# The last tile of a layer gets its own staging buffers and a 53-partition store, in a three-layer GNN kernel on one core

## What is computed

```
for l in range(3):
    ht  = einsum('nd,rdo->nro', h, W_rel[l])              # a table of 16 rows per node
    h_rel = segment_sum(ht[src, etype], dst) + h @ W_loop[l] + b_rel[l]
    z = h @ W_gat[l];  el = sum(z*attn_l);  er = sum(z*attn_r)      # per head
    e = leaky_relu(el[src] + er[dst]);  alpha = softmax over the edges of dst
    h_gat = segment_sum(alpha * z[src], dst) + b_gat[l]
    hc = concat(h_rel, h_gat) @ W_fuse + b_fuse
    if l == 0: hc = hc * sigmoid(concat(hc, mean weight) @ W_gate + b_gate)
    h = relu(hc)
out = layernorm(x + h)
```

## Time and profile before

| | us |
|---|---|
| median of 3 runs (3658.16 to 3663.75) | 3663.73 |
| the profiled execution | 3656.87 |
| its span in the trace | 3655.3 |
| POOL busy / DVE busy | 2529.9 / 2408.4 |
| ACT busy / PE busy | 430.8 / 688.1 |

### The profile page before, as it was taken

One profiled execution on the slowest core, in us unless ns is written; L12 is line 12 of the kernel. 1 busy time (PEld: TensorE's weight loads), 2 busy tenths in 40 slices (PEclk: granted clock), 3 DMA queues, 4 the chain that ended last, 5 costly groups with the idle time before them and its releaser, 6 DMA issues.

```text
span 3655.3 us, 19643 instructions
## 1 busy us (share of the span) xinstructions
PE 688.1 (19%) x1896; PEld 364.2 (10%) x1896; DVE 2408.4 (66%) x3225; ACT 430.8 (12%) x844; POOL 2529.9 (69%) x2681
## 2 busy tenths in 40 slices
PE   6750111122212221011111112121000000000000
PEld 5420000011101110000000001010000000000000
DVE  6505767677666763676667756673676777877786
ACT  4350011111111111010111111111000000000000
POOL 0057777777777764777777777774777777777774
PEclk9885555555555555555555556565555555555555
DMA  5694454454445553555445445554533333333332
GB/s 203 233 357 99 128 150 150 150 150 150 150 150 160 161 165 113 111 146 150 150 150 150 150 153 169 150 169 134 107 105 105 106 105 104 104 105 105 104 104 58
DMA packets 153683, 517.16 MB, mean 141 GB/s; under 512 B 47272, under 2 KB 54648, under 8 KB 140864
## 3 DMA queue, kind: packets, MB, share of 16 engines
q0 software_dynamic: 132384, 452.73, 43.5%
q1 hardware_dynamic: 21280, 64.25, 4.8%
HBM read 351.66 MB, written 165.18 MB: 141 GB/s over the span
## 4 chain that ended last, share of the span: by engine, by line
POOL 46%; issue 30%; DVE 9%; DMA 5%; PE 3%; POOLq 3%; DVEq 1%; SPq 1%; ACT 0%; ACTq 0%; PEldq 0%
POOL meta_nat L611 19%; POOL late L611 15%; POOL scratch L611 10%; DVE acc L1382 3%; DMA scratch<-table,stage_tail 1%; DMA late<-table,stage_mid 1%; PE ps_table L919 1%; DVE late L1378 1%; DVE scratch L1378 1%; PE ps_cnt L970 1%; POOL table L690 1%; POOLq L353 1%; DMA meta_nat<-table,stage_head 1%; POOL ell L575 1%; POOL meta_ranked L565 1%
## 5 line engine op out<-in xcount | busy, mean ns | idle before, releaser
L611 POOL DMA_INDIRECT meta_nat<-table,stage_head x1200 | 1137.8, 948 | 393.6 <-issue 371.9
L611 POOL DMA_INDIRECT late<-table,stage_mid x768 | 727.4, 947 | 233.9 <-issue 232.4
L611 POOL DMA_INDIRECT scratch<-table,stage_tail x558 | 528.8, 948 | 172.9 <-issue 172.3
L1061 PE MATMUL ps_mix<-ident,hr 128*128 128x128 f32 x75 | 35.4, 472 | 2121.8 <-DVE hg L1401 2121.8
L823 ACT ACTIVATE ps_cnt<-logit 128x68 f32<-128x68 f32 x192 | 44.4, 231 | 2947.3 <-DVE logit L1364 2947.3
L1382 DVE TENSOR_REDUCE acc<-meta_nat 128x132 f32<-128x2112 f32 x75 | 291.2, 3883 | 7.7
L1372 DVE TENSOR_REDUCE acc<-meta_nat 128x128 f32<-128x2048 f32 x75 | 283.1, 3775 | 0.0
L1085 PE MATMUL ps_table<-wrel,hT 128*128 128x512 f32 x400 | 270.1, 838 | 0.0
L1354 DVE TENSOR_TENSOR raw<-late,er_cur 128x64 f32<-128x64 f32 x48 | 12.8, 267 | 372.2 <-DMA late<-table,stage_mid 372.2
L1061 PEld LDWEIGHTS ps_mix<-ident,hr 128*128 128x128 f32 x75 | 13.6, 181 | 2171.0 <-DVE hg L1401 2171.0
L1354 DVE TENSOR_TENSOR raw<-meta_nat,er_cur 128x64 f32<-128x64 f32 x75 | 20.0, 266 | 304.8 <-DMA meta_nat<-table,stage_head 302.2
(11 more groups left out here) (187 smaller groups left out, 1771.6 us busy)
## 6 DMA issues: line engine op xcount, KB each, us to landing
table<-rows SPq DMA_DIRECT2D x50, 1040.0 KB, 5.8
meta_nat<-table,stage_head POOLq DMA_INDIRECT x1200, 2.8
late<-table,stage_mid POOLq DMA_INDIRECT x768, 2.8
scratch<-table,stage_tail POOLq DMA_INDIRECT x558, 2.8
meta<-meta_ranked POOLq DMA_DIRECT2D x1, 3250.0 KB, 30.1
xin<-in_x SPq DMA_DIRECT2D x48, 64.0 KB, 4.4
table<-rows,stage_id POOLq DMA_INDIRECT x50, 7.9
late<-in_dst SPq DMA_DIRECT2D x1, 402.8 KB
```

The source lines that it names most:

```text
L611: pool.indirect_dma_start(out=slots[b][:, k, :], out_offset=None, in_=table[l % 2], in_offset=bass.IndirectOffsetOnAxis(ap=index, axis=0)) ...
L1061: pe.transpose(mix[0], hr[:], ident[:])
```

## The change

Four edits. `stage_id` and `yo` become lists of two; the last tile of a layer uses `rows[1]`, `stage_id[1]` and `yo[1]` (`home=1`), and no longer waits for the store before it. The last tile's store takes partitions 0 to 52 (`held = N - (T - 1) * P`), in both forms of `store_tile`. The 75 x 16 rows of no node in `table[1]` are therefore cleared once in the prologue, out of `null_row`, with one more DMA of POOL. In `next_rows` ACT copies e_r in front of the two copies of messages.

```
@@ prologue, POOL
             pool.dma_start(table[1][NULL:NULL + 1, :], null_row[0:1, :]).then_inc(s_out, 16)
+            pool.dma_start(table[1][N * R:NP_ * R, :].rearrange("(p r) f -> p r f", r=R),
+                           null_row[0:NP_ - N, :].rearrange("p (o f) -> p o f", o=1).to_broadcast([NP_ - N, R, ROW])
+                           ).then_inc(s_spare, 16)
...
+            pool.wait_ge(s_spare, 16)
@@ store_tile
-            def store_tile(l, nth=None):
+            def store_tile(l, nth=None, home=0, held=P):
...
-                        out_offset=bass.IndirectOffsetOnAxis(ap=stage_id[:], axis=0),
-                        in_=rows[0][:].rearrange("p r f -> p (r f)"), in_offset=None).then_inc(s_stored, 16)
+                        out_offset=bass.IndirectOffsetOnAxis(ap=stage_id[home][0:held], axis=0),
+                        in_=rows[home][0:held].rearrange("p r f -> p (r f)"), in_offset=None).then_inc(s_stored, 16)
...
-                        out=out, out_offset=bass.IndirectOffsetOnAxis(ap=stage_id[:], axis=0),
-                        in_=yo[:], in_offset=None, bounds_check=N - 1, oob_is_err=False).then_inc(s_out, 16)
+                        out=out, out_offset=bass.IndirectOffsetOnAxis(ap=stage_id[home][0:held], axis=0),
+                        in_=yo[home][0:held], in_offset=None, bounds_check=N - 1, oob_is_err=False).then_inc(s_out, 16)
...
-                store_tile(l, nth=T)
+                store_tile(l, nth=T, home=1, held=N - (T - 1) * P)
@@ next_rows (ACT)
-                    act.wait_ge(s_stored, n_stored)
+                    if home == 0:
+                        act.wait_ge(s_stored, n_stored)
...
-                    s.activation(rows[0][:, :, D:ROW], bc(ps_z[:, 0:D + H], R), ACT.Copy)
+                    s.activation(rows[home][:, :, D:ROW], bc(ps_z[:, 0:D + H], R), ACT.Copy)
+                    s.activation(meta[:, bass.ds(t, 1), M_ER:M_X],
+                                 ps_z[:, D + H:ZW].rearrange("p (o f) -> p o f", o=1), ACT.Copy)
...
-                    s.activation(meta[:, bass.ds(t, 1), M_ER:M_X],
-                                 ps_z[:, D + H:ZW].rearrange("p (o f) -> p o f", o=1), ACT.Copy).then_inc(s_rows, 1)
+                    e.then_inc(s_rows, 1)
@@ epilogue (DVE), last tile: home=1
-                    dve.wait_ge(s_out, n_out)
-                    dve.reg_add(n_out, n_out, 16)
+                    if home == 0:
+                        dve.wait_ge(s_out, n_out)
+                        dve.reg_add(n_out, n_out, 16)
...
-                dve.wait_ge(s_stored, n_stored)
+                if home == 0:
+                    dve.wait_ge(s_stored, n_stored)
```

More of the change, by code:

```diff
@@ L200, in gnn_kernel @@
         stage_hub = sb("stage_hub", [P, PAIR], U32)
-        stage_id = sb("stage_id", [P, 1], U32)
+        stage_id = [sb(f"stage_id{i}", [P, 1], U32) for i in range(2)]
         blk_start = sb("blk_start", [P, 1])
@@ L221, in gnn_kernel @@
         y = sb("y", [P, D])
-        yo = sb("yo", [P, D])
+        yo = [sb(f"yo{i}", [P, D]) for i in range(2)]
         stats = sb("stats", [P, 6])
@@ L296, in gnn_kernel @@
         s_stored = sem("rows_stored")
+        s_spare = sem("rows_of_no_node_cleared")
         s_uns = sem("order_flag_ready")
@@ L843, in gate, with next_rows @@
                 act.reg_add(n_e, n_e, 1)
-            def next_rows(l, t):
+            def next_rows(l, t, home=0):
                 if l < L - 1:
-                    act.wait_ge(s_stored, n_stored)
+                    if home == 0:
+                        act.wait_ge(s_stored, n_stored)
                     act.reg_add(n_stored, n_stored, 16)
                     act.wait_ge(s_z_ps, n_tab)
-                    s.activation(rows[0][:, :, D:ROW], bc(ps_z[:, 0:D + H], R), ACT.Copy)
+                    s.activation(rows[home][:, :, D:ROW], bc(ps_z[:, 0:D + H], R), ACT.Copy)
+                    s.activation(meta[:, bass.ds(t, 1), M_ER:M_X],
+                                 ps_z[:, D + H:ZW].rearrange("p (o f) -> p o f", o=1), ACT.Copy)
                     for j in range(2):
                         act.wait_ge(s_chunk[2 * j + 1], n_tab)
-                        s.activation(rows[0][:, j * R // 2:(j + 1) * R // 2, 0:D],
-                                     ps_table[:, 1024 * j:1024 * j + 1024].rearrange("p (r f) -> p r f", f=D), ACT.Copy)
-                    s.activation(meta[:, bass.ds(t, 1), M_ER:M_X],
-                                 ps_z[:, D + H:ZW].rearrange("p (o f) -> p o f", o=1), ACT.Copy).then_inc(s_rows, 1)
+                        e = s.activation(rows[home][:, j * R // 2:(j + 1) * R // 2, 0:D],
+                                         ps_table[:, 1024 * j:1024 * j + 1024].rearrange("p (r f) -> p r f", f=D),
+                                         ACT.Copy)
+                    e.then_inc(s_rows, 1)
                     act.reg_add(n_tab, n_tab, 1)
@@ L899, in _ @@
                 gate(l)
-                next_rows(l, T - 1)
+                next_rows(l, T - 1, home=1)
         @block.tensor
@@ L1409, in norm_step, with epilogue @@
                 dve.reg_add(n_norm, n_norm, 1)
-            def epilogue(l, t):
+            def epilogue(l, t, home=0):
                 if l == 0:
@@ L1424, in epilogue @@
                         norm_step(v.tensor_tensor(nv[:, 0:1], nv[:, 0:1], nv[:, 1:2], ALU.mult))
-                    dve.wait_ge(s_out, n_out)
-                    dve.reg_add(n_out, n_out, 16)
-                    v.tensor_scalar(yo[:], y[:], mv[:, 0:1], nv[:, 0:1], ALU.subtract, ALU.mult).then_inc(s_yo, 1)
+                    if home == 0:
+                        dve.wait_ge(s_out, n_out)
+                        dve.reg_add(n_out, n_out, 16)
+                    v.tensor_scalar(yo[home][:], y[:], mv[:, 0:1], nv[:, 0:1], ALU.subtract, ALU.mult).then_inc(s_yo, 1)
                 else:
@@ L1431, in epilogue @@
                     dve.reg_add(n_T, n_T, 1)
-                dve.wait_ge(s_stored, n_stored)
+                if home == 0:
+                    dve.wait_ge(s_stored, n_stored)
                 if l < L - 1:
                     dve.reg_add(n_stored, n_stored, 16)
-                v.tensor_copy(stage_id[:].bitcast(I32), id_u[:, bass.ds(t, 1)].bitcast(I32)).then_inc(s_id, 1)
+                v.tensor_copy(stage_id[home][:].bitcast(I32), id_u[:, bass.ds(t, 1)].bitcast(I32)).then_inc(s_id, 1)
             def norm_statistics(l, t):
@@ L1500, in _ @@
                     tile(l, t)
-                epilogue(l, T - 1)
+                epilogue(l, T - 1, home=1)
 _INS = ['x', 'src', 'dst', 'edge_type_16', 'edge_weight', 'L0_gnn_W_rel', 'L0_gnn_b_rel', 'L0_gnn_W_loop',
```

## The result

| | before | after |
|---|---|---|
| median | 3661.95 us (4 runs) | 3727.23 us (4 runs, 3727.18 to 3728.88) |
| ratio | | 1.0181, 95% interval [1.0163, 1.0198] |
| profiled run, its span | 3656.87, 3655.3 us | 3727.18, 3725.6 us |

The change made the kernel 65 us slower by the medians, 70 by the two profiled executions. The forecast of 3660 was wrong; what happened is rival 1, somewhat above its price (3717 and 3724 were worked out).

What follows compares the result with a forecast made beforehand. Gather issue was taken to pace layers, with savings possible at layer ends; -5.0 (stores) -0.4 (e_r) -0.6 (issue) +3.6 (clearing) = -2.4 us, giving 3654.5 or 3661.3, stated as 3660; whole range 3650 to 3727.

Steps and rivals of the forecast that it cites:

- rival 1: Last tile's stores: one engine carries all 53 rows, +56.7 us for two tables, +60.3 in all; chance 0.36.
- What bounds the kernel: Gather issue paces layers; at ends of layers 0 and 1, savings between products and next gather count whole, twice.
- The wait that is removed: Layer end: copying z without waiting for the earlier store gains 0, since PE's products are the path.
- e_r in front: Layer end: copying e_r before the messages fits ACT's wait for PE; 0.2 us less at each of two ends.
- The store of 53 partitions: Last tile's table store: rows spread over 14 engines, at most 4 each, 2.5 us less per end, 5.0 in all.
- Issuing 53: POOL's issue of the last tile's three stores: fewer indices save 0.2 us each, 0.6 in all.
- Clearing: Prologue: the added POOL DMA delays the third tile of x, carried to the first gather; +3.6 us.
- The store into `out`: End of last layer, within rival 1: 53 rows of 512 bytes in 6.6 packets one after another, +1.0 us.
- Rival 2: Last tile's stores: rows keep their engines, so the -5.0 falls away, +2.6 us in all; chance 0.24.
- Rivals 3 and 4: Store spread and clearing hidden, -6.0 us, chance 0.06; clearing on few engines, store won or not, +0 to +7, chance 0.05.

Runs made afterwards that it cites:

- e11: The changed kernel again, unmodified, run beside the kernel before on one chip: 3721.75 us against 3657.07, ratio 1.0177.
- e3: Changed kernel with 128 partitions in the last tile's stores and no clearing, leaving own buffers and e_r in front: 4127.09 us, ratio 1.0006 to the kernel before.
- e2: Changed kernel with 54 partitions in place of 53 in the last tile's stores: 4128.74 us (one run).
- e1: Changed kernel with 64 partitions (0 to 63) in place of 53 in the last tile's stores: 4134.63 us, ratio 1.0005 to the kernel before.
- e5: Changed kernel with the last tile's nodes in partitions 32 to 84, storing 64 partitions (32 to 95): 4137.75 us, ratio 1.0021 to the kernel before.
- e4: Kernel before with only the clearing DMA and its wait added: 4137.68 us, ratio 1.0007 to the kernel before.
- e8: The changed kernel again, unmodified, on the slower chip: 4209.34 us (one run), 78 over the kernel before there.
- e6: As e5, with the clearing issued late by SP behind its last store of layer 0's table: 4129.65 us against 4131.36 before, ratio 0.9994.
- e7: 128 partitions, no clearing, last tile's table store split into two DMAs of 8 rows per node: 4128.59 us, ratio 0.9995 to the kernel before.

## Why the prediction was wrong, step by step

**What bounds the kernel: right.** Everything between the products and the next gather went whole into the time, twice. The terms add up to 63.6 of e11's 63.9 us over the span of before.

**The wait that is removed, 0: right.** ACT idles 2.00 us ahead of the copy of z instead of 2.67, released by PE, and the messages wait for PE as before. e3 holds this edit without the others that matter, and shows nothing beside e_r's 0.17.

**e_r in front, 0.2 at each end: right in e3** (0.17), and gone in the change: the piece of POOL's issue ahead of the store is 0.64 + 0.23 us for 53 partitions in the chain above, and is 0.51 + 0.19 in the chain of before at the same place. 2.06 against 2.07 us is what is left.

**The store of 53 partitions, 5.0 less: this is the step that failed**, where it says "The store is POOL's, so I take the spread, and of the two spreads the first." It weighed two rows, SP's five engines for 125 partitions and POOL's nearly ten, and chose by the engine that issues. The kind of DMA was the difference that it passed over: the earlier trace rows are a direct copy, the store is indirect. e2 against the changed kernel shows which rule the indirect one follows: 54 go over nine engines, 53 over one. The price of rival 1 was right, 28.4 at each end for 29.2 and 28.5 measured, 28.1 and 27.9 of it transfer. By the Trainium skill, DMA: Bandwidth & Descriptors, section "Why a DMA increments its semaphore by 16 and not by 1", the number of engines is the largest up to 16 that divides the slowest dimension. The prediction named this as what speaks most against the change and gave the exception, which does not name indirect DMAs, the larger chance; 53, 54, 64 and 128 partitions all came out by the rule.

The same step had a second error, which the first hides. It counted rows per engine and took the 0.63 us of a row as fixed. e1 has the rows on all engines, and no gain; e5, with the same packets and bytes from partitions 32 to 95, has all of it. So a row costs 0.63 us when the 16 engines read from partitions on both sides of 64, and 1.29 when they all read from 0 to 63; one engine alone has 0.63 there too (the changed kernel), nine have 0.87 (e2). The 64 rows of e1 are 64 x 16640 bytes in 82.5 / 16 = 5.2 us, 206 GB/s; the 128 of the earlier trace rows go at 423 in 5.04 us, twice as fast. This agrees with the Trainium skill, SBUF — State Buffer, section "Door 1: The DMA port swizzle (why [64,N] ≈ [32,N])": partitions 0 to 63 reach half of the 16 ports, and the bit worth 64 picks the other half. The prediction asked of the 53 partitions only on which engines they lie, not whether all engines can read from them at the full rate. Even with a number that divides well the forecast's -5.0 would, by these rows, not have come from partitions 0 to 52.

**Issuing 53, 0.6 less: wrong in sign.** 1.58 instead of 0.98 us, with 54 partitions 0.95 and with 64 0.92 (e2, e1). It is not the number of indices that makes it dear. That it comes with the one engine is what the rows show; why is open. It is not free at the ends of layers: the first row of the store starts 2.65 and 2.15 us behind the issue, where it was 1.55 and 1.53. So 1.1 and 0.6 us of the two ends are not transfer.

**Clearing, +3.6: close in size, but by another way than the sum had.** The third tile of x came 3.6 us later in e4 and 4.7 in the change. The forecast had all of it as engine time of the two transfers. Of the 4.7 only 1.9 are a longer load; 2.8 are its later issue, since SP is held up in issuing the edge arrays. That 3.6 came so near is in part luck. It was to be carried to the first gather whole, and the rows allow that: on the chip of e1 to e8 the first gather is at 281.07, 281.50 and 282.45 without the early clearing (e3, e6, e7) and at 283.12 to 286.72 with it (e4, e1, e2, e8, e5), 3.6 apart by the means; in the change it is 4.0. The forecast took the clearing as a fixed price; e6 shows that it is only the place: issued behind the loads it costs nothing that the rows show.

**The store into `out`, +1.0 in rival 1: too small.** It cost 1.8, and 0.15 ahead of the issue. The term had the rows' own time alone; the issue is 0.6 dearer, and the landing takes 4.0 us where it took 2.2.

**The rivals.** Rival 1 decided; over its sum of 60.3 the measured terms have 0.4 more at the first gather, 0.9 at the output and 1.0 at the two stores, and the 0.4 of e_r and the 0.6 of issue were not gained: 63.6. The top of the stated range, 3727, does not come out of its own words either: rival 1 against the median with a clearing of 5.0 is 3725.4, and the measured median, 3727.23, is above both. Rival 2 is what e1 looks like, for another reason than its own: the rows do not keep their engines, they change their rate. Rivals 3 and 4 did not come.

**Open:** why single first gathers of one prologue lie up to 2.8 us apart, what the 6.7 us inside the layers are, why e5 is slower than its rows say, why an issue to one engine takes 1.58 us, how the clearing holds up SP's issuing, and whether 56 or 60 partitions (14 and 15 engines by the same rule) would do better than 64 from the same place, which I did not try.

## What to carry to other kernels

Before a DMA is made smaller by taking fewer partitions, look at two things: the largest divisor up to 16 of their number, which is how many engines carry it, and whether they lie on both sides of partition 64. A few unused rows more (64 in place of 53) are cheaper than a number without a large divisor. When two rows of a trace disagree on how something unseen will go, choose by the kind of operation, not by who issues it, and if a written rule fits one of them and the exception does not name your case, give the rule the larger chance.

## What the runs showed of the hardware that was not expected

- An indirect DMA of 53 partitions sent all its rows through one engine (53 x 0.63 us), one of 54 through nine; each round of rows put one small packet on every idle engine (811 = 16 + 53 x 15, 58 = 16 + 6 x 7).
- A store of 64 rows took 82.5 us of engine time from partitions 0 to 63 and 40.6 from 32 to 95; one engine alone read rows of partitions 0 to 52 at the full 0.63 us each.
- Issuing the 53-partition store took POOL 1.58 us, those of 54, 64 and 128 took 0.95, 0.92 and 0.98; its first row started 2.65 us behind the issue instead of 1.55.
- A large DMA that POOL issued at 7 us held up SP's issuing: `late<-in_src` took SP 6.86 us instead of 3.27 (6.56 in e4, 3.31 in e3).
- A second indirect store directly behind a first reached its issue sooner: 1.3 us after the last copy's start instead of 1.9.
